# Three edits around the weights' blocks in the attention stage of a decoder layer: order of GpSimd's work, place of the blocks, and SP's store one pair later

## The chip, the cores and the metric

The kernel runs on one core of a Trainium2 chip (trn2). The metric is the device time of one execution in microseconds (us). The kernel before took 3059.69 us (median of three runs, 3051.11 to 3061.35).

The engines are named as in the profile: PE (TensorE, matmul) with PEld (its weight loads), DVE (VectorE), ACT (ScalarE), POOL (GpSimd) and SP (SyncE, which issues all DMA transfers here). Each runs its own instructions in order and waits on semaphores for the others.

## The reference

A decoder layer over x of shape (4, 512, 1024), in float32, in three steps, each followed by a layernorm of x plus the step's result:

```python
x = layernorm(x + attn(x, ...))          # down-projection, two Hydra state-space passes, up-projection
x = layernorm(x + xattn(x, ctx, ...))    # cross-attention on 1601 context rows, 16 heads
x = layernorm(x + ffn(x, ...))           # gated FFN, weights of 4-bit integers with scale and zero point

def xattn(Q, K, Wq_d, W_qk, Wkv_d, Wv_u):
    C_q, C_kv = Q @ Wq_d, K @ Wkv_d                       # 128 and 64 wide
    scores = einsum('bnhl,bkl->bhnk', (C_q @ W_qk).reshape(b, n, 16, 64), C_kv) / 8
    V_up = (C_kv @ Wv_u).reshape(b, nkv, 16, 64)
    return einsum('bhnk,bkhd->bnhd', softmax(scores), V_up).reshape(b, n, 1024)

def dequantize(w, s, z):                                  # groups of 128 rows
    return (w - repeat(z, 128)) * repeat(s, 128)
def ffn(x, ...):
    return (silu(x @ gate) * (x @ up)) @ down             # 1024 -> 3584 -> 1024
```

## The kernel before

Three stages follow each other with a barrier between them: `mixer` (from the start to about 398 us), `attention` (to about 1709 us) and `ffn` (the rest). The change touches `attention` alone.

**Attention.** There are 4 batches with 16 heads, and each head has 4 tiles of 128 query rows. One tile of one head is a unit (256 units), two units are a pair (128 pairs, 32 for each batch). For a unit PE multiplies the queries with the keys in two halves of the 1601 context rows (`scores`, L869), DVE takes the negated maximum (`maximum`, L1043), ACT takes the exponent of both halves (`exponent`, L957), DVE transposes the first 1280 columns in 32x32 squares into `b_tn` (`turn`, L1051, the instruction at L1055), and PE transposes the other three tiles of 128 (`turn`, L910), which ACT copies (L971). The squares have to be brought to other partitions. For a pair, 16 quarters of 32 partitions go from `b_tn` to `b_pt`: GpSimd copies six of them (`blocks`, L1141, the instruction at L1147), ACT one (`cross`, L977), and SP moves nine by DMA (`exchange`, L781, the issues at L787). Then PE multiplies all with the latent context (`weigh`, L890, the matmuls at L905). It waits for all three (`moved`, L763), and so does DVE before it writes to the same `b_tn` again two pairs later.

All engines walk over the units in one order written out by hand (PE L930, ACT L996, DVE L1110). At step k PE does the second half of the scores of unit k, then one of the two parts of `weigh` (for unit k-5 and its neighbour, so the first part of pair p comes at step 2p+5), then the transposes of unit k-1 and the first half of the scores of unit k+1. Every fourth and eighth step has a projection of queries or of outputs.

**The weights' blocks.** The integer weights of the FFN are prepared during this stage: 84 blocks of 128x1024 (`BLOCKS`, 28 each of gate, up and down). SP loads a block `b_rw` and its zero points `b_rz`, 512 KB each as written (`load`, L790). GpSimd subtracts and then casts to the matmul's type in place (`prepare`, L1169, instructions at L1171 and L1173). SP stores it (`store`, L799). `b_rw` has two buffers, `b_rz` one. `block_of` (L682) puts 21 blocks on the first 21 pairs of each batch, and the other 11 pairs have none.

**Order on SP** (L828): for each pair the nine transfers of `exchange`, then, where the pair has a block i, `store(i)`, which waits for the cast of block i, and `load(i + 1)`; behind them the keys of a later batch at two places, and rows of the normalised output (stored at pairs 23 to 26 of a batch) and of the next input (loaded at pairs 27 to 30).

**Order on GpSimd** (L1177): for each pair `prepare`, then the six copies, then in odd pairs the sums of the softmax (L1154) and the addition of a head's output (L1162); in pairs 20 to 23 of batches 1 to 3 a normalisation (L1166), and in pair 2 of batches 1 and 2 the splitting of a batch's keys in a high and a low part (L1137, L1139).

Of the kernel before, what the change touches and what calls it, by code (L numbers as in the profile page):

```python
# [6 lines left out]
I32 = mybir.dt.int32  # L7
ALU = mybir.AluOpType
# [3 lines left out]
P = 128  # L12
L, NB = 4, 512
TOK = L * NB
HID = 1024
# [649 lines left out]
PAIRS = 2 * NHEAD  # L665
# [7 lines left out]
NBLK = INTER // P  # L673
BLOCKS = [(n, j) for j in range(NBLK) for n in "gud"]
PER_BATCH = len(BLOCKS) // L
LN_SLOTS = [15, 16, 19, 20, 23, 24, 27, 28]
LN_VAR, LN_FACTORS, LN_PAIR, STORE_PAIR = 31, 35, 20, 23
WEIGH_AT = 5
# [2 lines left out]

def block_of(p):  # L682
    b, n = p // (PAIRS // L), p % (PAIRS // L)
    return b * PER_BATCH + n if n < PER_BATCH else None


def ring_events():
# [17 lines left out]
def attention(nc, d, kvd, cq, ident, shared, raw, wint, x1, x2):  # L705

    with ExitStack() as ctx:
        def sb(name, shape, dt=F32):
            return ctx.enter_context(nc.sbuf_tensor(name, shape, dt))
# [29 lines left out]
        ot = sb("b_ot", [P, NB])  # L739
        yo = sb("b_yo", [P, 2, QT, LAT])  # L740
        rw = [sb(f"b_rw{j}", [P, HID], I32) for j in range(2)]
        rz = sb("b_rz", [P, HID], I32)
        nm = sb("b_nm", [P, 2])
        den = sb("b_den", [P, 2, QT, 2])
        rd = sb("b_rd", [P, 2, QT])
# [34 lines left out]
        def sync():  # L780
# [9 lines left out]
            def load(i):  # L790
                n, j = BLOCKS[i]
                if i >= 2:
                    Q.wait_ge(s_wout[i % 2], 16 * (i // 2))
                Q.dma_start(rw[i % 2][:, :], raw[n + "w"][j, :, :]).then_inc(s_rin[i % 2], 16)
                if i:
                    Q.wait_ge(s_sub, i)
                Q.dma_start(rz[:, :], raw[n + "z"][j:j + 1, :].broadcast_to([P, HID])).then_inc(s_rin[i % 2], 16)

            def store(i):  # L799
                n, j = BLOCKS[i]  # L800
# [24 lines left out]
            for b in range(2):  # L825
                for q in range(QT):
                    load_rows(b, q)
            for p in range(PAIRS):  # L828
                exchange(p)
                i = block_of(p)  # L830
                if i is not None:
                    store(i)
                    if i + 1 < len(BLOCKS):
                        load(i + 1)
                if p in KEYS_LOAD:
                    Q.wait_ge(s_kl, KEYS_LOAD[p] - 1)
                    Q.wait_ge(s_cnp, 2 * (KEYS_LOAD[p] - 1))
                    load_keys(KEYS_LOAD[p])
                b, n = p // (PAIRS // L) - 1, p % (PAIRS // L) - STORE_PAIR
                if b >= 0 and 0 <= n < QT:  # L840
                    store_rows(b, n)
                if b >= 0 and b + 2 < L and QT <= n < 2 * QT:
                    load_rows(b + 2, n - QT)
            for q in range(QT):
                store_rows(L - 1, q)
            for k in range(2):
# [285 lines left out]
        def gpsimd():  # L1132
# [35 lines left out]

            def prepare(i):  # L1169
                G.wait_ge(s_rin[i % 2], 32 * (i // 2 + 1))  # L1170
                G.tensor_tensor(rw[i % 2][:, :], rw[i % 2][:, :], rz[:, :], ALU.subtract).then_inc(s_sub, 1)  # L1171
                G.wait_ge(s_sub, i + 1)
                G.tensor_copy(rw[i % 2][:, :].bitcast(F32R), rw[i % 2][:, :]).then_inc(s_cast, 1)  # L1173

            G.wait_ge(s_zero, 2)
            split_keys(1)
            for p in range(PAIRS + 4):  # L1177
                if p < PAIRS and block_of(p) is not None:
                    prepare(block_of(p))
                if p < PAIRS:  # L1180
                    blocks(p)
                if p % 2 and p < PAIRS:
                    sums(p // 2)
                if p % 2 and p >= 5:
                    output((p - 5) // 2)
                b, n = p // (PAIRS // L), p % (PAIRS // L)
                if 1 <= b < L and LN_PAIR <= n < LN_PAIR + QT:
                    normalise(b - 1, n - LN_PAIR)
                if n == 2 and 1 <= b <= 2:
                    split_keys(b + 1)  # L1190
# [402 lines left out]
```

## Time and profile before

| what | value |
|---|---|
| median of three runs | 3059.69 us (3051.11 to 3061.35) |
| the profiled execution | 3070.59 us, span 3068.8 us |
| mean granted PE clock | 0.948 of full speed |
| busy over the span | PE 88%, PEld 66%, DVE 75%, ACT 51%, POOL 67% |
| attention, 398 to 1709 us | PE busy 1108.8 us, POOL 913.0 us, clock 0.94, 187 GB/s |

The span runs from the first to the last instruction of the program. An engine's busy share says how long instructions ran on it, not that the kernel waited for it. A granted clock below 1 means that PE ran slower for a part of the time. DMA issues stand under SPq with the time that SP needed to issue them; a transfer lands later. In a list of instructions the bracket at the end tells how long the engine was idle before, and which work ended last before it went on. Where an instruction waits for several semaphores that attribution can name the wrong one, or say "issue".

### The profile page before, as it was taken

Reading aid. Unit: us, or ns where it says so; the run is one execution under the profiler, and the core shown is the slowest. Engines: PE = TensorE matmul, PEld = TensorE weight load, DVE = VectorE, ACT = ScalarE, POOL = GpSimd, SP = SyncE. Lnnn points to the kernel's source line nnn. Section 1 sums busy time; section 2 is a strip of 40 time slices with the busy share of each in tenths; the row PEclk is TensorE's granted clock in tenths of the full one; section 3 lists DMA queues with packets and bytes.
Section 4 is the critical chain, followed back from the end, with each engine's and each line's share of the span. In section 5 each row is a group of like instructions: output and inputs, shape, how many; then the busy total and the mean of one; then the engine's idle time right before and its main releaser. Section 6 shows DMA issues by size and latency. Waiting matters only on the chain. (4 is left out here: it accounts for less than half of the span.)

```text
span 3068.8 us, 41059 instructions
## 1 busy us (share of the span) xinstructions
PE 2694.8 (88%) x14296; PEld 2040.5 (66%) x14296; DVE 2293.6 (75%) x2167; ACT 1562.0 (51%) x2479; POOL 2046.0 (67%) x1559
## 2 busy tenths in 40 slices
PE   6776978898888987897889599999998699999997
PEld 3554755566556665665656478888887588888885
DVE  1526666677677776786767589999998589999998
ACT  2242555566556655675556445454543544545453
POOL 1000357766777677757775488888885588888883
PEclk9888989999999999999999799999999899999998
DMA  7304677755676576657764312222221322222221
GB/s 246 135 3 174 207 232 217 215 130 147 210 222 177 161 212 209 183 149 215 223 179 115 142 62 76 73 72 76 69 76 56 137 69 71 74 76 69 76 69 69
DMA packets 157870, 412.18 MB, mean 134 GB/s; under 512 B 29921, under 2 KB 49250, under 8 KB 157666
## 3 DMA queue, kind: packets, MB, share of 16 engines
q1 hardware_dynamic: 152802, 399.54, 42.1%
q10 hardware_dynamic: 4864, 10.03, 0.9%
q8 instruction: 115, 1.88, 0.3%
q14 instruction: 89, 0.73, 0.1%
HBM read 244.24 MB, written 70.85 MB: 103 GB/s over the span
## 5 line engine op out<-in xcount | busy, mean ns | idle before, releaser
L1049 DVE TENSOR_REDUCE b_nm<-b_sc 128x1 f32<-128x1604 f32 x256 | 468.0, 1828 | 303.8 <-PE b_sc L886 303.1
L1147 POOL COPY b_pt<-b_tn 32x640 f32<-32x640 f32 x768 | 548.3, 714 | 155.7 <-DVE b_tn L1055 116.2
L968 ACT ACTIVATE b_pr<-b_sc,b_nm 128x799 f32<-128x799 f32 (+1 forms) x512 | 476.7, 933 | 344.4 <-DVE b_nm L1049 266.3
L1428 DVE SCALAR_TENSOR_TENSOR c_acc<-c_ps,c_sd,c_acc 128x1024 f32<-128x1024 f32 x448 | 572.6, 1282 | 96.2 <-PE c_ps L1326 96.2
L1370 ACT ACTIVATE c_scaled<-c_ps,c_sgu 128x1024 f32<-128x1024 f32 x336 | 375.3, 1118 | 452.3 <-PE c_ps L1326 441.0
L905 PE MATMUL b_po<-b_pt,shared 128*64 128x256 f32 x2560 | 422.7, 419 | 148.4 <-issue 144.2
L1481 POOL TENSOR_TENSOR c_sum_u<-c_sum_u,c_scaled 128x1024 f32<-128x1024 f32 x168 | 404.6, 2408 | 79.5 <-ACT c_scaled L1370 78.6
L1481 POOL TENSOR_TENSOR c_sum_g<-c_sum_g,c_scaled 128x1024 f32<-128x1024 f32 x168 | 404.5, 2408 | 70.6 <-ACT c_scaled L1370 70.0
L886 PE MATMUL b_sc<-b_kh,b_qs 128*128 128x402 f32 (+1 forms) x1024 | 407.0, 398 | 39.3 <-ACT b_pr L968 35.7
L905 PEld LDWEIGHTS b_po<-b_pt,shared 128*64 128x64 f32 x2560 | 219.8, 145 | 299.3 <-issue 228.2
L1055 DVE STREAM_TRANSPOSE b_tn<-b_pr 128x1280 f32<-128x1280 f32 x256 | 385.1, 1504 | 43.3 <-POOL b_pt L1147 40.1
L886 PE MATMUL b_sc<-b_kl,b_qs 128*128 128x402 f32 (+1 forms) x1024 | 361.9, 353 | 0.0
L1171 POOL TENSOR_TENSOR b_rw<-b_rw,b_rz 128x1024 int32<-128x1024 int32 x84 | 199.3, 2372 | 206.4 <-DMA b_rz<-in_c_uz 93.2
L1428 DVE SCALAR_TENSOR_TENSOR c_sum_u<-c_ps,c_sgu,c_sum_u 128x1024 f32<-128x1024 f32 x224 | 285.8, 1276 | 31.7 <-POOL c_sum_u L1481 25.7
L1428 DVE SCALAR_TENSOR_TENSOR c_sum_g<-c_ps,c_sgu,c_sum_g 128x1024 f32<-128x1024 f32 x224 | 286.3, 1278 | 28.6 <-PE c_ps L1326 17.9
L1326 PE MATMUL c_ps<-c_hh,c_dw_int 128*128 128x512 f32 x896 | 281.8, 396 | 13.2 <-POOL c_hl L1497 13.2
L1326 PE MATMUL c_ps<-c_xh,c_uw_int 128*128 128x512 f32 x896 | 280.4, 394 | 13.1 <-DVE c_sum_u L1428 6.7
L1326 PE MATMUL c_ps<-c_xh,c_gw_int 128*128 128x512 f32 x896 | 278.8, 393 | 1.4 <-ACT c_sum_g L1370 1.3
L1326 PE MATMUL c_ps<-c_hl,c_dw_int 128*128 128x512 f32 x896 | 279.5, 393 | 0.0
L1326 PE MATMUL c_ps<-c_xl,c_uw_int 128*128 128x512 f32 x896 | 279.5, 393 | 0.0
L1326 PE MATMUL c_ps<-c_xl,c_gw_int 128*128 128x512 f32 x896 | 277.7, 391 | 0.0
L886 PEld LDWEIGHTS b_sc<-b_kh,b_qs 128*128 128x128 f32 x1024 | 200.5, 196 | 114.9 <-ACT b_pr L968 74.7
(181 smaller groups left out, 4158.0 us busy)
## 6 DMA issues: line engine op xcount, KB each, us to landing
b_pt<-b_tn SPq DMA_DIRECT2D x1152, 80.0 KB, 2.8
c_uw_int<-wint_u SPq DMA_DIRECT2D x56, 512.0 KB, 3.4
c_gw_int<-wint_g SPq DMA_DIRECT2D x56, 512.0 KB, 3.4
c_dw_int<-wint_d SPq DMA_DIRECT2D x56, 512.0 KB, 3.4
a_cx<-in_b_ctxT SPq DMA_DIRECT2D x16, 1608.0 KB, 11.4
b_rw<-in_c_gw SPq DMA_DIRECT2D x28, 512.0 KB, 4.6
b_rz<-in_c_gz SPq DMA_DIRECT2D x28, 512.0 KB, 6.2
wint_g<-b_rw SPq DMA_DIRECT2D x28, 512.0 KB, 3.0
```

Source lines behind the costliest of these rows:

```text
L886: ins = T.matmul(sc[:, at:at + n], qs[g // 2 % 2][:, g % 2, q * P:(q + 1) * P], k[b % 2][:, k0:k0 + n], start=(z == 0), stop=(z == 1))
L905: ins = T.matmul(po[z * LAT:(z + 1) * LAT, s * 256:(s + 1) * 256], cn[:, b, t, :], turned, start=(t < 2), stop=(t >= NKT - 2))
L968: S.activation(pr[u % 2][:, k0:k1], sc[:, at + lo:at + hi], ACT.Exp, bias=nm[:, u % 2:u % 2 + 1], accum_out=den[:, g % 2, q, half:half + 1 ...
L1049: V.tensor_reduce(nm[:, u % 2:u % 2 + 1], both, AXY, ALU.max, negate=True).then_inc(s_nm, 1)
L1055: V.transpose(tn[u // 2 % 2][:, :, u % 2, :], pr[u % 2][:, 0:4 * SEG].rearrange("p (c e) -> p c e", c=4)).then_inc(s_tt, 1)
L1147: G.tensor_copy(pt[s][32 * c:32 * c + 32, a, :, :], tn[s][32 * a:32 * a + 32, c, :, :]).then_inc(s_block, 1)
L1171: G.tensor_tensor(rw[i % 2][:, :], rw[i % 2][:, :], rz[:, :], ALU.subtract).then_inc(s_sub, 1)
L1326: ins = T.matmul(pair[slot % 4][:, b * 512:(b + 1) * 512], w[n][t % 2][:, k * P:(k + 1) * P], v[:, b * 512:(b + 1) * 512], start=(z == 0), ...
L1370: S.activation(dst[:, :], pair[SLOT[x, j] % 4][:, :], ACT.Identity, scale=scale(x, j)).then_inc(s_e, 1)
L1428: V.scalar_tensor_tensor(out=total, in0=pair[SLOT[x, j] % 4][:, :], scalar=scale(x, j), in1=total, op0=ALU.mult, op1=ALU.add).then_inc(s_a ...
L1481: G.tensor_tensor(total, total, scaled[m % 2][:, :], ALU.add).then_inc(s_add, 1)
```

## The change

1. `block_of` no longer uses pairs 0 to 20 of a batch but all pairs that are not in `FREE` (2, 5, 8, 11, 14, 17, 20 to 23, 27). There are 21 blocks in each batch as before; the longest run of neighbouring pairs with a block is 28 to 31 with 0 and 1 of the next batch. The last block falls in the last pair.
2. The zero points have two buffers, and `load(i)` waits for the subtraction of block i-2 instead of i-1 before it writes one.
3. On SP, the store of the block of pair p-1 comes at the head of pair p, before its exchange. The load of the next block follows the exchange. The store of the last block follows the loop.
4. On GpSimd, the copies of a pair, the sums and the output's addition come first, then the block's subtraction and cast.

```diff
+FREE = (2, 5, 8, 11, 14, 17, 20, 21, 22, 23, 27)
+BUSY = [n for n in range(PAIRS // L) if n not in FREE]
@@ def block_of(p):
     b, n = p // (PAIRS // L), p % (PAIRS // L)
-    return b * PER_BATCH + n if n < PER_BATCH else None
+    return b * PER_BATCH + BUSY.index(n) if n in BUSY else None
@@ def attention
-        rz = sb("b_rz", [P, HID], I32)
+        rz = [sb(f"b_rz{j}", [P, HID], I32) for j in range(2)]
@@ def load(i):
                 Q.dma_start(rw[i % 2][:, :], raw[n + "w"][j, :, :]).then_inc(s_rin[i % 2], 16)
-                if i:
-                    Q.wait_ge(s_sub, i)
-                Q.dma_start(rz[:, :], raw[n + "z"][j:j + 1, :].broadcast_to([P, HID])).then_inc(s_rin[i % 2], 16)
+                if i >= 2:
+                    Q.wait_ge(s_sub, i - 1)
+                Q.dma_start(rz[i % 2][:, :], raw[n + "z"][j:j + 1, :].broadcast_to([P, HID])).then_inc(s_rin[i % 2], 16)
@@ SP
             for p in range(PAIRS):
+                if p and block_of(p - 1) is not None:
+                    store(block_of(p - 1))
                 exchange(p)
                 i = block_of(p)
-                if i is not None:
-                    store(i)
-                    if i + 1 < len(BLOCKS):
-                        load(i + 1)
+                if i is not None and i + 1 < len(BLOCKS):
+                    load(i + 1)
...
+            store(len(BLOCKS) - 1)
             for q in range(QT):
                 store_rows(L - 1, q)
@@ GpSimd
-                G.tensor_tensor(rw[i % 2][:, :], rw[i % 2][:, :], rz[:, :], ALU.subtract).then_inc(s_sub, 1)
+                G.tensor_tensor(rw[i % 2][:, :], rw[i % 2][:, :], rz[i % 2][:, :], ALU.subtract).then_inc(s_sub, 1)
@@ GpSimd
             for p in range(PAIRS + 4):
-                if p < PAIRS and block_of(p) is not None:
-                    prepare(block_of(p))
                 if p < PAIRS:
                     blocks(p)
                 if p % 2 and p < PAIRS:
                     sums(p // 2)
                 if p % 2 and p >= 5:
                     output((p - 5) // 2)
+                if p < PAIRS and block_of(p) is not None:
+                    prepare(block_of(p))
```

## Rows read from the trace of the kernel before

**Rows 1.** The chain that ended last, in order of time: start, us, what.
```profile
1709.00 6.18 DMA c_xs<-x
```
**Rows 2.** DVE's transposes (L1055): duration ns min/median/max, first and last start us.
```profile
L1055 DVE STREAM_TRANSPOSE b_tn<-b_pr x256: 1495/1502/1514, 398.3 to 1676.1; 128x1280 f32<-128x1280 f32 x128
```
**Rows 3.** Two windows: length, busy of PE, PEld, DVE, ACT, POOL (count), PEclk, DMA, GB/s.
```profile
773.55:933.92 160.37, 131.12 (x808) 92.65 (x807) 114.68 (x98) 92.11 (x183) 120.68 (x134) 0.95 0.71 216
985.84:1037.14 51.30, 50.12 (x318) 34.23 (x317) 43.44 (x34) 35.99 (x75) 28.35 (x43) 1.00 0.54 151
```
**Rows 4.** DVE in order of time, second transposes of pairs: start, us, engine, instruction.
```profile
984.22 1.50 DVE L1055 STREAM_TRANSPOSE b_tn<-b_pr 128x1280 f32<-128x1280 f32 x1
...
993.74 1.50 DVE L1055 STREAM_TRANSPOSE b_tn<-b_pr 128x1280 f32<-128x1280 f32 x1
...
1001.63 1.50 DVE L1055 STREAM_TRANSPOSE b_tn<-b_pr 128x1280 f32<-128x1280 f32 x1
...
1010.35 1.50 DVE L1055 STREAM_TRANSPOSE b_tn<-b_pr 128x1280 f32<-128x1280 f32 x1
...
1018.10 1.50 DVE L1055 STREAM_TRANSPOSE b_tn<-b_pr 128x1280 f32<-128x1280 f32 x1
```
**Rows 5.** POOL in order of time, an odd pair with a block.
```profile
827.24 2.37 POOL L1171 TENSOR_TENSOR b_rw<-b_rw,b_rz 128x1024 int32<-128x1024 int32 x1 [2.57 <-DMA b_rz<-in_c_gz]
829.66 1.04 POOL L1173 CAST b_rw<-b_rw 128x1024 fp32r<-128x1024 int32 x1
830.64 4.59 POOL L1147 COPY b_pt<-b_tn 32x640 f32<-32x640 f32 x6
...
835.47 0.73 POOL L1162 TENSOR_TENSOR b_y<-b_y,b_yo 128x256 f32<-128x256 f32 x1
838.52 2.36 POOL L1171 TENSOR_TENSOR b_rw<-b_rw,b_rz 128x1024 int32<-128x1024 int32 x1 [2.32 <-DMA b_rz<-in_c_uz]
```
**Rows 6.** PE in order of time, the first products over that pair's quarters.
```profile
835.34 1.91 PE L905 MATMUL b_po<-b_pt,shared 128*64 128x256 f32 x14 [2.22 <-issue]
```
**Rows 7.** SP's issues in order of time beside it: store, weights, zero points, exchange.
```profile
830.73 0.33 SPq L802 DMA_DIRECT2D wint_g<-b_rw  x1
831.40 0.33 SPq L794 DMA_DIRECT2D b_rw<-in_c_uw  x1
831.78 0.58 SPq L797 DMA_DIRECT2D b_rz<-in_c_uz  x1
832.59 5.60 SPq L787 DMA_DIRECT2D b_pt<-b_tn  x9
```
**Rows 8.** Groups of instructions: the subtraction's waits; landing times of the zero points (L797).
```profile
L1171 POOL TENSOR_TENSOR b_rw<-b_rw,b_rz 128x1024 int32<-128x1024 int32 x84 | 199.3, 2372 | 206.4 <-DMA b_rz<-in_c_uz 93.2 <-DMA b_rz<-in_c_dz 62.7 <-DMA b_rz<-in_c_gz 50.5
...
DMA to landing us min/median/max: 5.4/6.2/8.1
```
**Rows 9.** PE in order of time, free stretch, first products of the pairs of rows 4.
```profile
995.73 1.94 PE L905 MATMUL b_po<-b_pt,shared 128*64 128x256 f32 x14
...
1003.84 1.94 PE L905 MATMUL b_po<-b_pt,shared 128*64 128x256 f32 x14
...
1012.18 1.94 PE L905 MATMUL b_po<-b_pt,shared 128*64 128x256 f32 x14
...
1021.28 1.94 PE L905 MATMUL b_po<-b_pt,shared 128*64 128x256 f32 x14
```
**Rows 10.** Landing times of the exchange (L787): 1046 to 1275 us, then 1290 to 1372.
```profile
DMA to landing us min/median/max: 2.0/3.3/5.4
...
DMA to landing us min/median/max: 2.0/2.1/3.6
```
**Rows 11.** POOL in order of time, the splitting of a batch's keys.
```profile
755.87 1.52 POOL L1137 CAST b_kh<-shared 128x1601 fp32r<-128x1601 f32 x1
757.47 3.62 POOL L1139 TENSOR_TENSOR b_kl<-shared,b_kh 128x1601 fp32r<-128x1601 f32 x1
```
**Rows 12.** DVE in order of time, one of the statistics.
```profile
836.87 0.65 DVE L1071 BATCH_NORM_STATS2 b_stats<-b_y 128x6 f32<-128x512 f32 x1
```

## The prediction

> **What bounds the kernel now.** The chain of waits ends in the last stage: its first long piece starts at 1709.00 us, where the input of that stage lands [rows 1]. Before that a barrier cuts it, so the chain says nothing of the attention stage, where the whole change lies. That stage has to be read from its own windows.
>
> I read first how long it takes. DVE's 256 transposes (two for each of the 128 pairs) start from 398.3 to 1676.1 us [rows 2]: 1277.8 us for 127.5 pairs, 10.02 us for each. Next, two windows side by side [rows 3]. From 773.55 to 933.92 each pair carries a weights' block: 15 pairs in 160.37 us, 10.69 each, PE busy 131.12 of 160.37 us, granted clock 0.95, DMA share 0.71. From 985.84 to 1037.14 no pair has one: PE is busy 50.12 of 51.30 us at clock 1.00. DVE's transposes start at 984.22 and four pairs later at 1018.10 [rows 4]: 33.88 us, 8.47 a pair. So 84 of 128 pairs pay about 2.2 us each for their block (less the odd longer stall), and there is a rhythm without blocks that is known.
>
> Why do they pay? GpSimd's rows of one pair with a block [rows 5]: the subtraction starts at 827.24 after 2.57 us of waiting for the zero points, the cast follows at 829.66, and only then, at 830.64, the six copies of the pair's quarters (4.59 us), until 835.23. PE's first product over these quarters starts at 835.34, after 2.22 us idle [rows 6]: it waited for GpSimd, though the row says "issue" (it waits for several semaphores). And the zero points? SP's rows [rows 7] have the store of this block at 830.73, right after the cast, the next block's weights at 831.40, its zero points at 831.78. The latter land in 6.2 us (median, 5.4 to 8.1) [rows 8], and the next subtraction starts at 838.52 [rows 5]. So there is a ring of one pair: cast, store, load (1.2 us of issuing), landing 6.2, subtraction and cast 3.4: 10.8, against 10.69 measured. The load stands behind the store in SP's queue, and the store waits for the cast. GpSimd's wait for zero points is 206.4 us in 78 places [rows 8], the size of the whole gap between 10.02 and 8.47 (197.9 us over 127.5 pairs).
>
> **The change, part by part.**
>
> *Store one pair later, load no longer behind the cast.* In pair p SP issues the store of the block before, the nine transfers of exchange(p), then the next load. The second zero-point buffer is needed for that: with one, the load would wait for this pair's subtraction. The ring above is cut: the load leaves after the exchange, whatever GpSimd does.
>
> *Copies ahead of the block on GpSimd.* PE no longer waits for subtraction and cast (3.4 us) in front of the copies. The copies need 4.6 us from the transposes' end; PE wants them at the earliest 8.6 us after it (below), so 4.0 us of delay are covered.
>
> *Does the loaded block arrive in time?* With T the end of a pair's transposes: the exchange takes SP 5.60 us [rows 7], the weights' issue 0.5, the zero points go at T+6.2, landed T+12.4. GpSimd wants them at the next pair (8.5 later) behind its copies (4.65): T+13.1, and T+14.1 where the odd pair's sum and output (0.97, from 835.23 to 836.20) come before. Just in time at the median; with the longest landing 1 us late, which touches only the block, not the pair.
>
> *GpSimd's time.* An even pair with block is 4.65+3.4 = 8.1 us, an odd one 9.1; the mean of 8.6 is 0.1 over the rhythm, but every third pair is without one, so three pairs need at most 4.65x3+3.4x2+0.97x2 = 22.7 of 25.4. Lag doesn't add up, except in the six blocks of pairs 28 to 31, 0 and 1, by well under 1 us.
>
> *The wait that is added.* The store now stands ahead of the exchange and waits for the cast of the pair before. Queued behind it on SP: nine transfers, then the load; PE waits for the transfers and DVE's transposes two pairs on wait for PE. How much cover is there? In the free stretch transposes end at 985.72, 995.24, 1003.13 and 1011.85 [rows 4] and PE's first product of the same pairs starts at 995.73, 1003.84, 1012.18, 1021.28 [rows 9]: 10.0, 8.6, 9.05 and 9.4 us later. Nothing held PE there, so these are the times at which it comes by. An exchange from T is issued by T+5.6 and its last transfer, issued at T+5.0, lands 2.1 later (median of the free stretch) at T+7.1; beside blocks the median is 3.3, longest 5.4 [rows 10], so T+8.3; a part of the exchanges meets no block's transfer at its end, and I take 7.7, half way. The cover is then 0.9 to 2.3 us. The added wait: after an even pair the cast ends at 8.1 against a gap of 7.8 to 7.9, after an odd one at 9.1 against 8.7 or 9.5, plus up to 0.3 of lag and 0.4 for the store's issue: 0 to 1.15 us. The tightest class (8.6) has the smallest wait (0 to 0.35), since a gap of 9.5 lies before it; the others come to 8.3 to 8.9 against 9.05 to 10.0. So the medians are covered and only tails stick out. Price for the 84 pairs behind a block: at least 0, at most 1.0 each (longest wait and a landing at the 3.3 or above), taken 0.2 (nearer the covered medians): 17 us.
>
> One rule of the Trainium skill speaks against this order. In "DMA: Bandwidth & Descriptors", section "Queues, rings and completion order", it says that each DMA engine consumes the descriptors of one queue in ring order: the exchange's pieces stand behind the store just issued, and behind the load. The 3.3 us beside blocks against 2.1 without [rows 10] agree in direction. By the rows the order costs the 0.2 just taken; if every piece really waited for a whole store the first rival below would be the outcome.
>
> *Smaller terms.* In pair 2 of two batches GpSimd splits keys, 1.52+3.62 us [rows 11]; it makes the next block's cast late by about 2 us, and through the store the next exchange: 2.5 each (0 to 4), 5 us. Rows stored and loaded by SP, one issue each (0.58, as the zero points, of the same size [rows 7]), now share pairs with blocks, about 12 times, half hidden: 3 us. In the last pairs the gap is shorter and the store of pair 126's block holds the last exchange: 1.5 us; the last block itself (3.4 us) lies beside the final projection. SP's issue per pair with block is 0.33+5.60+0.33+0.58 and gaps, 7.1 us of 8.47, not the bound. DVE's statistics (0.65 each, eight a batch [rows 12]) lay beside GpSimd's waits before; in the free stretch DVE has 51.30-43.44 = 7.9 us idle over six pairs [rows 3], 1.3 a pair, which takes one of them: no cost, and 24x0.65 = 16 us at most if none were hidden (a part of the range).
>
> **Sum.** Ceiling 197.9 (all pairs at 8.47); less 17, 5, 3 and 1.5: a gain of 171.4 us. The profiled execution took 3070.6 us (span 3068.8 and 1.8 around it), so 2899.2; its like in the runs is the median 3059.7, 10.9 lower, so 2888, said 2889. Stages one and three stay as they are.
>
> **Rivals.**
> 1. *The exchange comes late behind store and load* (chance 0.14). For: the 3.3 against 2.1 us. Against: before, store and both loads were issued right ahead of an exchange as well, and the price is then already in the 7.7. If it lands at T+10.3 with the wait, each pair behind a block stretches by about 1.0: 84 instead of 17, gain 104: 2955.
> 2. *Everything is covered* (0.14): only the tail and half of the splits are left (4 us), gain 194: 2866. For: medians fit in every class. Against: landings scatter up to 5.4.
> 3. *The load is still late* (0.04): zero points of the block in the second of two neighbouring pairs land after T+14. At the longest landing (8.1) 42 blocks are late by 1 to 2 us, their stores and so the exchanges too: 42x1.2 = 50 beyond the 17, gain 121: 2938. The change then does only half of what its order of issue promises.
> 4. *Slower than before* (0.03): the new loop store, exchange, PE, transposes, copies, block, store closes. It takes 0.4+7.7 for the exchange, 7.9 from PE's start to the transposes two pairs on (995.73 to 1003.13 is 7.4), 9.1 on GpSimd: 25.1 for three pairs, while three pairs have 25.4. It is thus nearly closed already, and what is added to it counts in full. The gain is gone when each of the 84 pairs pays 2.3 us, that is when exchanges land 3 to 4 us later than the 7.7 taken, around T+12 with the wait. At 2.8 us each: 235-198+9 more = 3106. Against it: in rows 10 no single landing is above 5.4, which makes T+10.4.
>
> **How the numbers follow.** Forecast 0.65 (faster, 2889, own range 2872 to 2920), rivals as above. Below 2862 nothing can lie, were the free rhythm the floor; I set the range 2864 to 2950, which leaves out the upper half of rival 1 and rival 4. Runs of this kernel scatter by 10 us, and 0.3% (9 us) is about what can be told from no change. Faster holds forecast and rivals 1 to 3, 0.96 less the chance that their prices add up; 0.95. Same 0.02, slower 0.03.
>
> **What would show it.** Right: the 256 transposes start over about 1105 us; GpSimd's idle time before its subtraction falls from 206 us to below 30 while before its copies it grows (it waits for DVE); the granted clock of the stage rises from 0.94 towards 1.00; PE's waits before the first product over the quarters are under 1 us. Wrong: pairs with blocks stay at 9.5 us or more, with waits of PE for the exchange's transfers, or SP waiting for the cast for over 1 us in most pairs; or the subtraction still waits for its zero points by some us in each pair.

## The result, and the profile after

The changed kernel took 2911.22 us (median of four runs, 2907.49 to 2918.31), the kernel before beside it 3060.52; the ratio is 0.9521 with a 95% interval of 0.9493 to 0.9548. The forecast was 2889 with a range of 2864 to 2950: direction and mechanism came out, the gain was 149 us where 171 was said. In the two profiled executions (3070.59 and 2909.64 us) the difference is 161 us; 10 us of that is that the profiled execution of the kernel before is slower than its median.

First the views of the changed kernel that answer those at the head of the prediction. DVE's transposes (the line is now L1058; duration ns, first and last start), the answer to [rows 2]:

```profile
L1058 DVE STREAM_TRANSPOSE b_tn<-b_pr x256: 1495/1502/1514, 399.3 to 1520.2; 128x1280 f32<-128x1280 f32 x128
```

They start over 1120.9 us in place of 1277.8: 156.9 us of the 161.0 by which the span shrank (3068.8 to 2907.8). The rest is the last stage, in which nothing was changed and which is 8 us shorter here, less a tail of the attention stage that is 3 us longer and a first stage that is 1 us longer. The 8 us look like scatter: over the 14 traces kept here the last stage lasts 1347 to 1360 us, and this one of the kernel before has the longest. The windows of the three stages, the second ending about 7 us before its stage does (length, busy of PE, PEld, DVE, ACT, POOL, then PE's granted clock, DMA share, GB/s):

```profile
0.00:398.00 398.00, 301.47 (x1708) 206.90 (x1709) 179.02 (x367) 140.66 (x308) 39.36 (x22) 0.89 0.45 152
398.00:1549.00 1151.00, 1068.65 (x6958) 738.49 (x6956) 940.08 (x769) 766.30 (x1543) 916.58 (x1082) 0.99 0.70 212
1549.00:2907.80 1358.80, 1278.21 (x5632) 1051.93 (x5632) 1175.04 (x1032) 651.66 (x628) 1093.34 (x456) 0.97 0.24 79
```

In the attention stage PE is now busy 93% of the time, at clock 0.99. The gaps closed, and the granted clock rose with them from 0.94: PE's own busy time there fell from 1108.8 to 1068.7 us without one matmul less. Now the groups that waited, the answers to [rows 8] and to PE's first products (busy and mean ns, then the idle time before them and what ended it):

```profile
L1174 POOL TENSOR_TENSOR b_rw<-b_rw,b_rz 128x1024 int32<-128x1024 int32 x84 | 198.8, 2367 | 9.2 <-DMA b_rz<-in_c_uz 3.9 <-DMA b_rz<-in_c_gz 1.4 <-DMA b_rz<-in_c_dz 0.7
L908 PE MATMUL b_po<-b_pt,shared 128*64 128x256 f32 x2560 | 391.3, 394 | 31.7 <-DMA b_pt<-b_tn 31.4
L1150 POOL COPY b_pt<-b_tn 32x640 f32<-32x640 f32 x768 | 550.3, 717 | 199.3 <-DVE b_tn L1058 159.3
```

GpSimd's wait for zero points fell from 206.4 to 9.2 us. Before its copies it is now idle for 199.3 us in place of 155.7 and waits mostly for DVE, which is where an engine off the path should wait. PE's idle time before the products over quarters was 148.4 us and is 31.7, and what ends it has changed. Before, the profile put 144.2 us of it down to "issue"; all of that lies at 75 pairs, at which PE starts within 0.25 us behind GpSimd's last copy, so it was GpSimd. Now it is the exchange's transfers. The row of the kernel before:

```profile
L905 PE MATMUL b_po<-b_pt,shared 128*64 128x256 f32 x2560 | 422.7, 419 | 148.4 <-issue 144.2 <-DMA b_pt<-b_tn 4.2
```

How GpSimd works now, an odd pair and the even one behind it, in order of time; the answer to [rows 5]:

```profile
851.65 4.61 POOL L1150 COPY b_pt<-b_tn 32x640 f32<-32x640 f32 x6
856.35 0.20 POOL L1157 TENSOR_TENSOR b_rd<-b_den 128x4 f32<-128x4 f32 x1
856.50 0.73 POOL L1165 TENSOR_TENSOR b_y<-b_y,b_yo 128x256 f32<-128x256 f32 x1
857.18 2.37 POOL L1174 TENSOR_TENSOR b_rw<-b_rw,b_rz 128x1024 int32<-128x1024 int32 x1
859.61 1.04 POOL L1176 CAST b_rw<-b_rw 128x1024 fp32r<-128x1024 int32 x1
860.60 4.61 POOL L1150 COPY b_pt<-b_tn 32x640 f32<-32x640 f32 x6
```

Copies, output, block and the next copies follow without a gap: 8.95 us from copies to copies, the forecast was 9.1. And SP's queue beside it, the answer to [rows 7] (start, us, line; nine issues merged in the exchange's rows):

```profile
851.74 0.33 SPq L804 DMA_DIRECT2D wint_g<-b_rw  x1
852.16 6.51 SPq L789 DMA_DIRECT2D b_pt<-b_tn  x9
858.72 0.58 SPq L796 DMA_DIRECT2D b_rw<-in_c_dw  x1
859.34 0.43 SPq L799 DMA_DIRECT2D b_rz<-in_c_dz  x1
860.68 0.33 SPq L804 DMA_DIRECT2D wint_u<-b_rw  x1
861.11 6.66 SPq L789 DMA_DIRECT2D b_pt<-b_tn  x9
```

The order is as said: store, exchange, load. The transposes of these pairs end at 851.39 and 860.11, so the exchanges start 0.77 and 1.00 us late, within the 0 to 1.15 of the prediction. Of the 83 exchanges right behind a store 66 start within 1.15 us (median 0.77), the others up to 3.61 us late. What was not foreseen is the 6.51 and 6.66 us that nine issues take in place of 5.60. Over the stage the exchange's issue takes 6.33 us on average (5.79 before), and issues of more than 0.8 us rose from 30 to 138. Of the 83 exchanges right behind a store 73 have such an issue, of the other 45 only 11. The last of the nine transfers lands 2.1 us (median) after its issue with or without a store ahead; what comes late is its issue. With a store ahead all nine have landed 9.4 us after the transposes (median; a quarter of them 10.2 or more), without one 7.1.

**Where the remaining time lies.** I measured each pair from the end of the second transposes of the pair before to the end of its own, and took off the free rhythm. That rhythm repeats over four pairs: 7.90, 8.71, 7.75 and 9.52 us, the differences of the ends in [rows 4] and of the following one, 33.88 together. Summed over the batches:

| pairs of a batch | priced by the prediction at | over the rhythm, changed kernel |
|---|---|---|
| 25 to 31, 0, 1 (rows and keys on SP, long run of blocks) | 3 for the rows, and a part of the 17 | 19.5 |
| 17 (square root of the norm, two table loads on ACT) | 0 | 9.7 |
| 2 to 16 (splits, latent turns, statistics, late exchanges) | 5 for the splits, and a part of the 17 | 9.1 |
| 18 to 24 | a part of the 17 | 3.2 |
| all | 25 | 41.5 |

PE's 31.7 us of waiting are 17.8 in the first group, 7.1 in the last two pairs and 6.7 anywhere else. One place of the first group, pairs 26 and 27 of a batch; SP first, then PE's first products:

```profile
1193.43 0.77 SPq L813 DMA_DIRECT2D x<-b_y  x1
1194.24 0.43 SPq L804 DMA_DIRECT2D wint_g<-b_rw  x1
1194.77 8.12 SPq L789 DMA_DIRECT2D b_pt<-b_tn  x9
1202.93 0.58 SPq L796 DMA_DIRECT2D b_rw<-in_c_dw  x1
1203.56 0.44 SPq L799 DMA_DIRECT2D b_rz<-in_c_dz  x1
1204.04 0.43 SPq L813 DMA_DIRECT2D x<-b_y  x1
1204.52 0.43 SPq L804 DMA_DIRECT2D wint_u<-b_rw  x1
1205.05 8.62 SPq L789 DMA_DIRECT2D b_pt<-b_tn  x9
```

```profile
1194.24 1.94 PE L908 MATMUL b_po<-b_pt,shared 128*64 128x256 f32 x14 [0.16 <-DMA b_pt<-b_tn]
1204.43 3.54 PE L908 MATMUL b_po<-b_pt,shared 128*64 128x256 f32 x14 [2.23 <-DMA b_pt<-b_tn]
1215.21 1.08 PE L908 MATMUL b_po<-b_pt,shared 128*64 128x256 f32 x8 [1.02 <-DMA b_pt<-b_tn]
```

SP issues without a pause between 1193.43 and 1213.67: for two pairs it needs more than 20 us, in a rhythm that gives it 17. PE waits 2.23 us for the first exchange. The second starts 3.61 us after its transposes (1201.44), and PE waits for it. Here SP is the bound.

And pair 17, the other group without a price. ACT, then DVE, in order of time:

```profile
820.47 1.28 ACT L996 ACT_TABLE_LOAD   x1
821.77 0.21 ACT L996 ACTIVATE b_rstd<-b_rstd 128x4 f32<-128x4 f32 x1
821.99 1.28 ACT L971 ACT_TABLE_LOAD   x1
823.29 0.93 ACT L971 ACTIVATE b_pr<-b_sc,b_nm 128x799 f32<-128x799 f32 x1
```

```profile
825.40 1.83 DVE L1052 TENSOR_REDUCE b_nm<-b_sc 128x1 f32<-128x1604 f32 x1 [2.04 <-PE b_sc L889]
...
828.57 0.14 DVE L1090 RECIPROCAL b_rstd<-b_rstd 128x4 f32<-128x4 f32 x1
828.74 2.05 DVE L1093 SCALAR_TENSOR_TENSOR b_nmr<-b_mv,b_rstd 128x4 f32<-128x4 f32 x1
```

ACT loads two tables in front of the next exponent. DVE's idle time before the maximum is 2.04 us, where it is 0.81 in pairs without the norm. And DVE's instruction on four numbers a partition takes 2.05 us (last section).

### The profile page after: what moved, and what is told of

It is laid out like the page before. It is cut to its first block and busy times, and to the rows that moved or that the text cites. A ratio compares the mean times of both kernels' runs of the same rounds, so it can differ in the third digit from the quotient of the medians.

```text
span 2907.8 us, 41065 instructions
## 1 busy us (share of the span) xinstructions
PE 2648.3 (91%) x14296; PEld 1997.3 (69%) x14296; DVE 2294.1 (79%) x2167; ACT 1558.6 (54%) x2479; POOL 2049.3 (70%) x1559
## 5 line engine op out<-in xcount | busy, mean ns | idle before, releaser
L1150 POOL COPY b_pt<-b_tn 32x640 f32<-32x640 f32 x768 | 550.3, 717 | 199.3 <-DVE b_tn L1058 159.3
L908 PE MATMUL b_po<-b_pt,shared 128*64 128x256 f32 x2560 | 391.3, 394 | 31.7 <-DMA b_pt<-b_tn 31.4
L1058 DVE STREAM_TRANSPOSE b_tn<-b_pr 128x1280 f32<-128x1280 f32 x256 | 384.8, 1503 | 3.3 <-DMA b_pt<-b_tn 1.3
L908 PEld LDWEIGHTS b_po<-b_pt,shared 128*64 128x64 f32 x2560 | 196.4, 138 | 181.6 <-DMA b_pt<-b_tn 54.3
L651 POOL TENSOR_TENSOR a_xt<-a_xt,a_bup 128x1024 f32<-128x1024 f32 x16 | 37.6, 2356 | 331.9 <-DMA a_xt<-in_a_x 276.2
```

The source lines that it names most:

```text
L651: G.tensor_tensor(xr[:, t % RING, :], xr[:, t % RING, :], bup[:, :], ALU.add).then_inc(s_bup, 1)
L908: ins = T.matmul(po[z * LAT:(z + 1) * LAT, s * 256:(s + 1) * 256], cn[:, b, t, :], turned, start=(t < 2), stop=(t >= NKT - 2))
L1058: V.transpose(tn[u // 2 % 2][:, :, u % 2, :], pr[u % 2][:, 0:4 * SEG].rearrange("p (c e) -> p c e", c=4)).then_inc(s_tt, 1)
L1150: G.tensor_copy(pt[s][32 * c:32 * c + 32, a, :, :], tn[s][32 * a:32 * a + 32, c, :, :]).then_inc(s_block, 1)
```

## The experiments

The medians, each with the ratio to the kernel before on the same chip; "stage" is from the first to the last start of the 256 transposes in the profile. e7, e8 and e13 leave out a part of the reference and serve only to price it. Ratios can be compared from row to row; where two intervals overlap, the difference of the times is not shown, and what is left is the profile.

| kernel | median us | ratio, 95% interval | stage us |
|---|---|---|---|
| before | 3060.52 | 1 | 1277.8 |
| changed | 2911.22 | 0.9521 (0.9493 to 0.9548) | 1120.9 |
| changed, second time | 2910.39 | 0.9521 (0.95 to 0.9543) | 1122.9 |
| e1, order on GpSimd alone | 3073.06 | 1.004 (1.0022 to 1.0059) | 1282.0 |
| e2, SP's order and buffers alone | 2965.2 | 0.9688 (0.9658 to 0.9718) | 1181.1 |
| e3, other pairs alone | 3066.48 | 1.0027 (1.0012 to 1.0042) | 1277.1 |
| e4, changed, blocks on pairs 0 to 20 | 2913.92 | 0.9529 (0.9509 to 0.9548) | 1128.5 |
| e5, changed, one zero-point buffer | 2915.7 | 0.9537 (0.9517 to 0.9558) | 1128.0 |
| e6, changed, store behind the exchange | 2905.79 | 0.9499 (0.948 to 0.9518) | 1117.5 |
| e7, changed, no square root | 2905.44 | 0.9503 (0.9484 to 0.9521) | 1110.5 |
| e8, changed, no subtraction and cast | 2896.14 | 0.947 (0.9444 to 0.9495) | 1105.1 |
| e9, changed, free pairs at the rows | 2902.31 | 0.9503 (0.9476 to 0.953) | 1112.0 |
| e10, e6 and e9 together | 2896.4 | 0.948 (0.9454 to 0.9505) | 1108.7 |
| e13, e10 without square root | 2884.76 | 0.9446 (0.9423 to 0.947) | 1100.1 |

### e1: the order on GpSimd alone

```diff
 (kernel before)
             for p in range(PAIRS + 4):
-                if p < PAIRS and block_of(p) is not None:
-                    prepare(block_of(p))
...
                 if p % 2 and p >= 5:
                     output((p - 5) // 2)
+                if p < PAIRS and block_of(p) is not None:
+                    prepare(block_of(p))
```

> The kernel before with one edit: on GpSimd the copies, sums and output come ahead of the block (blocks on pairs 0 to 20, one zero-point buffer, store and load as before). Theory (the ring cast, store, load, landing, subtraction and cast of 10.8 us sets the pair, and the load stands behind the store in SP's queue): the ring stays, and the exchange of the next pair still waits on SP behind the store; block pairs stay near 10.7 us, total 3045 to 3075. Rival (PE only suffers because the copies stand behind the block on GpSimd): the 3.4 us go out of PE's path, block pairs fall to 8.5 to 9, total 2890 to 2940.

Measured: 3073.06 us, 0.4% above the kernel before and inside the expected 3045 to 3075: no gain. The ring stays, and SP shows it, in order of time:

```profile
767.56 0.33 SPq L802 DMA_DIRECT2D wint_g<-b_rw  x1
767.94 0.43 SPq L794 DMA_DIRECT2D b_rw<-in_c_uw  x1
768.42 0.79 SPq L797 DMA_DIRECT2D b_rz<-in_c_uz  x1
769.30 5.60 SPq L787 DMA_DIRECT2D b_pt<-b_tn  x9
778.61 0.33 SPq L802 DMA_DIRECT2D wint_u<-b_rw  x1
```

From store to store 11.05 us. GpSimd's copies are early now, but the exchange of the next pair stands behind store and load, and PE waits for it instead. The group of its products in this kernel:

```profile
L905 PE MATMUL b_po<-b_pt,shared 128*64 128x256 f32 x2560 | 428.4, 423 | 148.6 <-DMA b_pt<-b_tn 145.1 <-POOL b_pt L1147 3.3
```

148.6 us of idle time as before (148.4), with another releaser. The exchange now starts 4.15 us (median) after its transposes, where it was 0.03. That GpSimd's order alone is the cause is refuted.

### e2: SP's order and the second zero-point buffer alone

```diff
 (changed kernel)
-BUSY = [n for n in range(PAIRS // L) if n not in FREE]
+BUSY = list(range(PER_BATCH))
...
             for p in range(PAIRS + 4):
+                if p < PAIRS and block_of(p) is not None:
+                    prepare(block_of(p))
...
-                if p < PAIRS and block_of(p) is not None:
-                    prepare(block_of(p))
```

> The kernel before with the SP edits alone: two zero-point buffers, the store one pair later, the load behind the exchange without waiting for this pair's cast; GpSimd still does the block ahead of the copies, blocks on pairs 0 to 20. Theory: the ring is cut, but landing (T+12.6), block (3.4) and copies (4.6) now lie in one chain to PE at T+20.7, 7.9 us ahead of the transposes two pairs on: 28.6 us for three pairs, 9.5 a block pair; total 2950 to 2985. Rival (only GpSimd's order counts): no change, 3045 to 3075.

Measured: 2965.2 us, inside the expected 2950 to 2985; pairs with a block take 9.64 us (9.5 expected). GpSimd, in order of time:

```profile
763.16 2.39 POOL L1174 TENSOR_TENSOR b_rw<-b_rw,b_rz 128x1024 int32<-128x1024 int32 x1 [2.78 <-DMA b_rz<-in_c_gz]
765.62 1.04 POOL L1176 CAST b_rw<-b_rw 128x1024 fp32r<-128x1024 int32 x1
766.60 4.59 POOL L1150 COPY b_pt<-b_tn 32x640 f32<-32x640 f32 x6
```

Copies end at 771.19 and PE's products start at 771.29. PE's idle time before the products is 79.1 us here, 75.3 of it right behind GpSimd's last copy. So cutting the ring gives 3.1%, and GpSimd's order, worth nothing by itself, gives another 1.6% once the ring is cut (e4, which differs from e2 in that order alone).

### e3 and e4: the pairs with blocks

```diff
 (e3: kernel before)
+FREE = (2, 5, 8, 11, 14, 17, 20, 21, 22, 23, 27)
+BUSY = [n for n in range(PAIRS // L) if n not in FREE]
-    return b * PER_BATCH + n if n < PER_BATCH else None
+    return b * PER_BATCH + BUSY.index(n) if n in BUSY else None
 (e4: changed kernel)
-BUSY = [n for n in range(PAIRS // L) if n not in FREE]
+BUSY = list(range(PER_BATCH))
```

> The kernel before with the blocks on the 21 pairs that the change uses, nothing else. Theory: a block costs when its load was issued only one pair ahead, that is in the 13 of 21 pairs of a batch whose neighbour ahead has a block too (20 of 21 before); at 2.4 to 3.3 us each 52 of them cost 125 to 170 us in place of 198: total 2985 to 3030. Rival (spreading is the whole gain): 2890 to 2930.

> The changed kernel with the blocks on pairs 0 to 20 again. Theory: with ring and order mended, 21 neighbouring pairs are bound by GpSimd (8.6 us a pair, 0.1 above the free rhythm) and by SP's added issue; block pairs take 8.7 to 9.1 us and the rows' pairs have no block: total 2905 to 2940, about as the changed kernel. Rival (spreading is needed, lag and DMA traffic add up): block pairs 9.5 and more, total 2975 and more.

Measured: e3 3066.48, e4 2913.92. My expectation for e3 was wrong: it gained nothing. I had priced a block with a block ahead at 2.4 to 3.3 us. In the profile of e3 three pairs with two blocks among them mostly lose 4 to 6.7 us together (2.5 to 7.7 over all), since GpSimd holds the copies of the second block's pair back until the load has landed, and the copies of the free pair behind it as well:

```profile
810.07 2.38 POOL L1173 TENSOR_TENSOR b_rw<-b_rw,b_rz 128x1024 int32<-128x1024 int32 x1 [9.14 <-DMA b_rz<-in_c_dz]
812.52 1.04 POOL L1175 CAST b_rw<-b_rw 128x1024 fp32r<-128x1024 int32 x1
813.50 4.59 POOL L1149 COPY b_pt<-b_tn 32x640 f32<-32x640 f32 x6
818.17 0.20 POOL L1156 TENSOR_TENSOR b_rd<-b_den 128x4 f32<-128x4 f32 x1
818.32 0.73 POOL L1164 TENSOR_TENSOR b_y<-b_y,b_yo 128x256 f32<-128x256 f32 x1
818.99 4.59 POOL L1149 COPY b_pt<-b_tn 32x640 f32<-32x640 f32 x6
```

In e4 pairs with a block take 9.02 us (8.7 to 9.1 expected) and the stage is 6 to 8 us longer than in the two profiles of the changed kernel, which the medians hardly show. The spreading, alone or on top of the rest, is worth between nothing and 8 us. Where the excess lies differs, though: in e4 pairs 25 to 31, 0 and 1, where only 0 and 1 have a block, stand 1.2 us under the rhythm in place of 19.5 over it, and the long run of blocks in pairs 2 to 24 pays 50 us in place of 22.

### e5: one zero-point buffer

```diff
 (changed kernel)
-        rz = [sb(f"b_rz{j}", [P, HID], I32) for j in range(2)]
+        rz = [sb("b_rz", [P, HID], I32)] * 2
-                if i >= 2:
-                    Q.wait_ge(s_sub, i - 1)
+                if i:
+                    Q.wait_ge(s_sub, i)
```

> The changed kernel with one zero-point buffer: the load of the next zero points waits for this pair's subtraction (done at T+7.1 in an even pair, T+8.1 in an odd one) in place of going at T+6.3. Theory: SP holds them back 0.8 to 1.8 us, they land at T+13.3 to 14.3, about when GpSimd comes by, but in pairs behind an even one the next exchange may start up to 0.3 us later: 2908 to 2925. Rival (the second buffer carries the gain): the load is a pair late, block pairs 10 us and more, over 3000.

Measured: 2915.7 us, inside the expected 2908 to 2925, and a ratio of 0.9537 whose interval overlaps that of the changed kernel (0.9521); its stage is 5 to 7 us longer in the profile. The second buffer brings at most those few us. So it is not needed for cutting the ring, as the prediction held.

### e6: the store behind the exchange

```diff
 (changed kernel)
-        rw = [sb(f"b_rw{j}", [P, HID], I32) for j in range(2)]
-        rz = [sb(f"b_rz{j}", [P, HID], I32) for j in range(2)]
+        rw = [sb(f"b_rw{j}", [P, HID], I32) for j in range(3)]
+        rz = [sb("b_rz", [P, HID], I32)] * 2
...
-                if p and block_of(p - 1) is not None:
-                    store(block_of(p - 1))
                 exchange(p)
                 i = block_of(p)
+                late = block_of(p - 1) if p else None
                 if i is not None and i + 1 < len(BLOCKS):
-                    load(i + 1)
+                    load(i + 1, late)
+                elif late is not None:
+                    store(late)
```

Left out of the diff: `load(i + 1, late)` issues the weights, then the store of block `late`, then, once the subtraction before is done, the zero points; before the weights it waits for all stores issued so far; and `rw[i % 2]` is `rw[i % 3]` everywhere.

> The changed kernel with three weight buffers and one zero-point buffer; SP issues in pair p the exchange, the next weights, then the store of the block before, then the zero points, so that no store stands right ahead of an exchange and no exchange waits for a cast. In the changed kernel 73 of the 83 exchanges right behind a store have an issue of over 0.8 us among their nine, 11 of the 44 others. Theory (the store right ahead delays the exchange by its wait and by stretching SP's issues, 26 us in the whole stage): exchanges are issued in 5.7 us on average in place of 6.3, PE's waits for the exchange fall from 31 us to about 12: 2890 to 2903. Rival (the long issues come from the traffic, wherever the store stands): no change, 2905 to 2920.

Measured: 2905.79 us, above the expected 2890 to 2903 and just inside the rival's 2905 to 2920. Long issues fell from 138 to 64 and the exchange's issue from 6.33 to 5.97 us on average, so about half of them come from the store right ahead. PE's waits fell only from 31.7 to 26.4, where about 12 was expected, since those at the rows (18.4 of them) stayed: of the 12 exchanges right behind the store of a row 10 have a long issue. That the store's place matters is shown in the issues; the effect on the time, 5 us by the medians, is within the intervals of both kernels.

### e7: no square root in the attention's norm

```diff
 (changed kernel)
-                S.activation(rstd[:, :], rstd[:, :], ACT.Sqrt).then_inc(s_std, 1)
+                S.copy(rstd[:, :], rstd[:, :]).then_inc(s_std, 1)
```

> The changed kernel with the square root of the attention's layernorm left out (a copy in its place), so that ACT loads no table for it. In the changed kernel pair 17 of batches 1 to 3 takes 10.59 us where the rhythm has 7.75, and the two table loads are 1.28 us each. Theory (they are on the path now, hidden under the blocks before): 3 x 2.6 = 7.7 us less, 2900 to 2906. Rival (DVE's scalar instruction that takes 2.05 us there in place of 0.16 is what costs): at most 2 us less, 2908 to 2915.

Measured: 2905.44 us, inside the expected 2900 to 2906; the stage is 10.4 us shorter, and pair 17 falls from 9.7 us over the rhythm to 1.2. Here DVE's scalar instruction takes 0.17 us again as well, so e7 alone doesn't separate the two. e8 does: there the table loads are left, the instruction takes 0.16 us in all batches, and pair 17 takes 9.35 us in batches 1 to 3. So does the profile of e6, in which nothing else is taken away: its pair 17 takes 10.60, 9.35 and 10.83 us in batches 1 to 3, with the instruction at 2.06, 0.16 and 2.28 us. Against the rhythm of 7.75 the tables are thus 1.6 us in each of three batches, 5 us in all, and the long instruction 1.25 us each, 4 us in all. The last 1.2 us are at pair 17 of batch 0, where there is no norm.

### e8: no subtraction and cast

```diff
 (changed kernel)
-                if p < PAIRS and block_of(p) is not None:
-                    prepare(block_of(p))
...
-                if i >= 2:
-                    Q.wait_ge(s_sub, i - 1)
...
             def store(i):
-                Q.wait_ge(s_cast, i + 1)
+                Q.wait_ge(s_rin[i % 2], 32 * (i // 2 + 1))
```

> The changed kernel without subtraction and cast: the blocks are stored as loaded, GpSimd does only the rest, the transfers are the same in number and size, and the store waits for the landing in place of the cast. Theory (what is left above the free rhythm is the traffic and SP's issues at the rows, the keys and behind stores, and the table loads; GpSimd's work itself is covered): 2893 to 2905. Rival (GpSimd's lag and the store's wait for the cast are the rest): all 24 us of PE's waits go, 2875 to 2888.

Measured: 2896.14 us, inside the theory's range. By the medians all of GpSimd's work on the blocks and the store's wait for the cast cost 15 us; the stage is 15.8 us shorter in a profile that is the fastest of runs from 2888 to 2909 us. 24.9 us over the rhythm remain, 6.0 of them at pair 17, and PE still waits 22.7 us for exchanges. So most of what remains is not GpSimd's work on the blocks. That it is the traffic and SP's issues is likely (122 issues are still over 0.8 us), but the two were not tried apart.

### e9, e10, e13 and the changed kernel again

```diff
 (e9: changed kernel; e10: e6)
-FREE = (2, 5, 8, 11, 14, 17, 20, 21, 22, 23, 27)
+FREE = (2, 5, 8, 11, 14, 17, 21, 23, 25, 27, 29)
 (e13: e10)
-                S.activation(rstd[:, :], rstd[:, :], ACT.Sqrt).then_inc(s_std, 1)
+                S.copy(rstd[:, :], rstd[:, :]).then_inc(s_std, 1)
```

> The changed kernel with other pairs without a block: 2, 5, 8, 11, 14, 17, 21, 23, 25, 27, 29 in place of 20 to 23 and 27, so that the pairs in which SP also moves rows and keys (23 to 30) hardly ever carry a block behind a block. In the changed kernel pairs 25 to 31 and 0 to 1 stand 19.5 us over the free rhythm, summed over the batches, and 25 of the 32 us of PE's waits for the exchange fall there (7 of them in the last two pairs). Theory (rows, keys and blocks in the same pairs fill SP's queue, which the sum priced at 3 us): those pairs fall to about 8 over, pairs 20 and 22 pay 1 to 2 for block and normalisation together; total 2896 to 2906. Rival (it is the traffic of the rows themselves, wherever the blocks are): 2908 to 2916.

> Both together: three weight buffers with the store behind the exchange and the next weights, one zero-point buffer, and the pairs without a block at 2, 5, 8, 11, 14, 17, 21, 23, 25, 27, 29. Theory: the two parts lie in different pairs and add up, and the shorter runs suit the one zero-point buffer; the store's part alone gave 5 us: 2890 to 2901. Rival (what one gives the other no longer finds): 2901 to 2906.

> The changed kernel itself once more, beside the next one on the same chip, since the single improvements (5 to 15 us) are near the scatter between chips. Theory and rival alike: 2905 to 2918.

> The kernel with three weight buffers, the store behind the exchange and the pairs without a block at the rows (measured 2896.4), with the square root of the attention's layernorm left out besides, so that ACT loads no table for it. Theory (the table loads lie on the path in that kernel as well, 10.0 us over the rhythm at pair 17 of batches 1 to 3): 6 to 9 us less, 2887 to 2891, and 0.94 to 0.945 of the kernel before; the rest to the free rhythm is then the keys, the latent turns and single late exchanges, about 20 us. Rival (the next late thing takes the place): 2893 to 2897.

Measured: e9 2902.31; its pairs 25 to 31, 0 and 1 fall from 19.5 to 4.3 us over the rhythm, its pairs 18 to 24 rise from 3.2 to 8.8. The expectation had about 8 for the first and 1 to 2 us a pair for the second. The stage is 9 us shorter than the changed kernel's, but the intervals of the ratios (0.9476 to 0.953, and 0.9493 to 0.9548) overlap. The group of PE's products in e9, then in e10:

```profile
L908 PE MATMUL b_po<-b_pt,shared 128*64 128x256 f32 x2560 | 390.4, 393 | 26.0 <-DMA b_pt<-b_tn 25.8
```

```profile
L914 PE MATMUL b_po<-b_pt,shared 128*64 128x256 f32 x2560 | 390.5, 393 | 17.5 <-DMA b_pt<-b_tn 17.4
```

e10 took 2896.4 us, inside the expected 2890 to 2901 and, by the medians, the sum of the two parts (5 and 9). It has the lowest median of the kernels here that compute the whole reference, 0.948 of the kernel before, and a stage 12 us shorter than the changed kernel's; the intervals of the two ratios still touch (up to 0.9505, and from 0.9493). The changed kernel took 2910.39 the second time, inside the expected 2905 to 2918. Beside it, on the same chip, e13 took 2884.76, below the expected 2887; the intervals 0.9423 to 0.947 and 0.95 to 0.9543 are apart.

## Why the prediction was right, and where it was off

- *The ring on SP and GpSimd sets the pairs with a block.* Shown: with the ring left in, nothing is gained by GpSimd's order (e1) or by other pairs (e3); with the ring cut and nothing else 3.1% is gained (e2).
- *Copies ahead of the block are covered.* Shown: of the 128 pairs' first products 75 started within 0.25 us behind GpSimd's last copy before, and none does now; 42 start right behind the exchange. GpSimd's 8.1 and 9.1 us for a pair with a block are 8.2 and 9.0 at the median.
- *The load arrives in time.* Yes: 9.2 us of waiting in all. Rival 3 is out.
- *The added wait of the store, priced at 17 us.* Its size was mostly right (median 0.77 us, 66 of 83 within the 0 to 1.15 said), and SP waited for the cast over 1 us at 35 of 84 stores, not at most of them. Its price was too high where no rows are moved: PE waits there 6.7 us in all. The price of all of GpSimd's block work, the wait included, is 15 us by the medians of e8; that this is near 17 is partly chance, for the 17 were 84 times a guess of 0.2 and the waits fell on few pairs.
- *When the exchange lands.* The prediction took the last transfer to land at the half way between 2.1 and 3.3 us after its issue. The 3.3 are the median of all nine transfers; the last one alone has 2.1 beside blocks too, in both kernels, while the first takes 4.7 (median) right behind a store. What moved the landing was the longer issue: 9.4 us after the transposes at the median, where 7.7 with 0 to 1.15 of wait, 8.9 at most, were said. Rival 1 named this delay, with T+10.3 and 84 us for it. Two thirds of that delay came, but not the price: PE's waits over the whole stage are 31.7 us. 13 pairs have a wait of over 1 us, where none was the sign of being right.
- *Rows stored and loaded by SP, priced at 3 us.* This is the term that was mis-sized: 19.5 us at the batches' ends, of which other free pairs take away 15, for 6 more in pairs 18 to 24 (e9). Rows without blocks beside them cost nothing there (e4, 1.2 us under the rhythm), and with the blocks' transfers but without GpSimd's work 13.7 of the 19.5 stay (e8): it is rows and blocks together in SP's queue. I had counted each row as one issue of 0.58 us. What I had not counted is that SP's issue of the exchange itself gets longer when stores are in front of it, 8.12 and 8.62 us in place of 5.60, so that its 7.1 us of a pair became more than the pair.
- *DVE's extra work, "no cost", and ACT's, not named.* 9.7 us at pair 17, of which 5 are ACT's table loads and 4 DVE's long instruction. I had named the statistics and left out both. The kernel before has both as well, in pairs that stood over the rhythm anyway; the free stretch from which I took the rhythm has no such step.
- *The ceiling, 197.9 us.* The rhythm held: between those places the pairs take 7.90, 8.71, 7.75 and 9.52 us to 0.03. The measured stage is 41.5 us above it where 25 were priced; that is 16 of the 22 us by which the forecast was too low. The rest is a tail longer by 3 us where 1.5 were said, and scatter. In the profiled executions alone the gain was 161 us, and only because the last stage was 8 us shorter does it come within 10 us of the 171; that part is luck.
- *The two parts that did not matter.* The prediction gave the spreading a role (every third pair lets GpSimd recover). e4 shows that 21 blocks in a row are as fast within 3 us of the median. It called the second zero-point buffer needed, since the load would wait for this pair's subtraction; e5 shows that this wait costs a few us at most.

## What to carry to other kernels

Read the rhythm in a stretch in which the cost is absent, and take as the ceiling what you get if all ran like that; then look for the steps that this stretch does not contain, since each of them comes out from under the cover. When a transfer's load stands behind its own store in one in-order queue, add up the ring of store, landing and work. If it is longer than the rhythm, as here (10.8 against 8.47 us), it is the bound, and here neither a different order on the worker nor other places for the work helped until it was cut. In a queue that issues for several purposes, count the time of all issues over the fullest pair, not the mean. Putting bulk stores behind the short transfers that someone waits for halved the long issues here; that it shortens the time is likely, not shown.

## What the runs showed of the hardware

**DMA issues get longer behind a bulk store.** One of the exchange's nine issues takes 0.59 us (median); with a 512 KB store issued right ahead one or two of the nine, mostly the second or third, take over 0.8 and up to 2.2 us. 30 long issues before, 138 after, 64 in e6. How soon the exchange follows matters: in the changed kernel it starts 0.1 us (median) after the store's issue is over, and 73 of 83 have a long issue; in e2, with the same order on SP, it starts 1.5 us after, and 42 of 84 do. Why they do was not tried.

**A DVE instruction of 0.16 us took 2.05 us beside GpSimd.** In the changed kernel it started at 828.74, and GpSimd's subtraction ran from 828.40 to 830.78. In e6 it started at 1108.47, ahead of the subtraction (1108.61), and took 0.16 us. The subtraction of the first, then both rows of e6:

```profile
828.40 2.38 POOL L1174 TENSOR_TENSOR b_rw<-b_rw,b_rz 128x1024 int32<-128x1024 int32 x1
...
1108.47 0.16 DVE L1099 SCALAR_TENSOR_TENSOR b_nmr<-b_mv,b_rstd 128x4 f32<-128x4 f32 x1
1108.61 2.36 POOL L1180 TENSOR_TENSOR b_rw<-b_rw,b_rz 128x1024 int32<-128x1024 int32 x1 [0.57 <-DMA b_rz<-in_c_dz]
```

DVE's ended at 830.79, with the subtraction. In every trace here in which it starts while a subtraction runs it ends 0.02 us behind it, whether it had 2.3 us to wait or 0.2; the kernel before has this too (1.82 and 0.87 us). The Trainium skill, page "SBUF — State Buffer", section "Who interferes with whom", says that a DVE instruction with two inputs in SBUF contends with a GpSimd instruction that reads SBUF, that the ports they share are an exclusive lock, and that the order of issue decides who blocks. The traces agree: this one reads the mean and the factor from SBUF; the transposes with one input keep their 1494 to 1516 ns in every run, and without the subtraction (e8) it takes 0.16. It cost about 4 us here (e6 and e8).

**The clock follows the gaps.** The stage ran at a granted clock of 0.94 before and 0.99 after (1 is the 2.4 GHz level), and the same products over quarters fell from 419 to 394 ns on average. From 420 to 1520 us the clock was 0.95 in e1 and 0.94 in e3, neither of which gained, 0.98 in e2, and 0.99 or 1.00 in all others. So some of the time saved is the clock's; PE's busy time fell by 40 us, and how much of that lay on the path was not separated.
